# Queries and keys of pairs 2 and 3: one projection and four taps on ScalarE and VectorE instead of four folded weight matrices

## The reference, cut to what matters

```python
def _short_conv(x, w):              # w: 128 channels x 4 taps
    xp = jnp.pad(x, ((0, 0), (3, 0), (0, 0)))
    y = sum((xp[:, t:t + L, :] * w[:, t] for t in range(4)))
    return jax.nn.silu(y)
q = _short_conv(hidden_states @ Wq.T, qconv_w)
k = _short_conv(hidden_states @ Wk.T, kconv_w)
v = _short_conv(hidden_states @ Wv.T, vconv_w)
```

## Time and profile before

| | us |
|---|---|
| three runs: median | 425.53 |
| three runs: lowest, highest | 421.48, 427.27 |
| profiled execution: its own time | 426.13 |
| profiled execution: span, first to last instruction | 424.4 |
| mean granted TensorE clock | 0.918 of full |

### The profile page before, as it was taken

The page is one execution under the profiler, slowest core; times in us unless marked ns, Lnnn a source line. Parts: engine busy times, 40 slices in busy tenths (PEclk is TensorE's granted clock), DMA queues, the critical chain, the costliest instruction groups (busy, mean ns, idle before and its releaser), DMA issues.

```text
span 424.4 us, 14279 instructions
## 1 busy us (share of the span) xinstructions
PE 344.0 (81%) x6364; PEld 253.7 (60%) x6364; DVE 276.2 (65%) x639; ACT 146.2 (34%) x264; POOL 90.2 (21%) x152
## 2 busy tenths in 40 slices
PE   7988977954657796888988869899897987867996
PEld 6344963643324565655776557477675755755885
DVE  3788931268747569767755797498739659667554
ACT  1342613301434351453413413533252353133221
POOL 4862000051622061440200715202000000200000
PEclk9699888968598779999999899899989899899999
DMA  7331350005120001110000011200000000000000
GB/s 255 124 94 29 40 123 19 5 3 129 15 37 4 3 2 28 15 25 14 5 2 2 26 29 15 38 3 3 2 28 4 2 0 0 2 25 2 0 2 25
DMA packets 42652, 12.47 MB, mean 29 GB/s; under 512 B 35424, under 2 KB 41696, under 8 KB 42464
## 3 DMA queue, kind: packets, MB, share of 16 engines
q1 hardware_dynamic: 39440, 9.47, 10.4%
q10 hardware_dynamic: 3152, 2.10, 1.6%
HBM read 8.68 MB, written 2.88 MB: 27 GB/s over the span
## 4 chain that ended last, share of the span: by engine, by line
PE 53%; DVE 24%; issue 8%; DMA 6%; ACT 4%; POOL 4%; SPq 0%; DVEq 0%; ACTq 0%
PE ps L546 17%; PE ps L585 12%; PE ps L441 9%; PE ps L485 7%; PE ps L471 3%; DVE x L1197 2%; DVE v_room L1186 2%; PE ps L614 2%; DMA a_d<-a_hc 2%; DMA t<-t_d 1%; DMA t_d<-t_it 1%; POOL t_it L386 1%; DVE toep_room L1230 1%; PE ps L633 1%; POOL rn L362 1%
## 5 line engine op out<-in xcount | busy, mean ns | idle before, releaser
L1186 DVE TENSOR_TENSOR v_room<-toep_room,ps 128x512 f32<-128x512 f32 x64 | 43.7, 684 | 44.1 <-PE ps L546 20.2
L585 PE MATMUL ps<-w_sb,v_room 128*128 128x128 f32 x512 | 64.9, 281 | 8.9 <-DVE x L1197 4.5
L585 PEld LDWEIGHTS ps<-w_sb,v_room 128*128 128x128 f32 x512 | 62.4, 195 | 14.3 <-issue 8.2
L546 PE MATMUL ps<-x_hi,w_sb 128*128 128x512 f32 x128 | 61.7, 482 | 4.0 <-DVE v_room L1186 2.6
L830 ACT ACTIVATE toep_room<-ps 128x512 f32<-128x512 f32 x64 | 38.1, 597 | 60.1 <-PE ps L546 56.6
L546 PE MATMUL ps<-x_lo,w_sb 128*128 128x512 f32 x128 | 52.4, 409 | 0.0
L546 PE MATMUL ps<-x_hi,w_lo 128*128 128x512 f32 x128 | 52.3, 409 | 0.0
L1197 DVE SCALAR_TENSOR_TENSOR x<-ps,rs,x 128x128 f32<-128x128 f32 x128 | 35.8, 342 | 16.5 <-PE ps L585 16.5
L362 POOL TENSOR_TENSOR rn<-ss,mh 128x16 f32<-128x16 f32 x8 | 23.1, 2901 | 65.1 <-DVE ss L1037 65.1
L396 POOL TENSOR_TENSOR g<-gm,mh 128x16 f32<-128x16 f32 x4 | 11.6, 2909 | 112.2 <-DVE gm L1298 112.2
L546 PEld LDWEIGHTS ps<-x_hi,w_sb 128*128 128x128 f32 x128 | 25.3, 198 | 13.3 <-DVE v_room L1186 3.6
(11 more groups left out here) (199 smaller groups left out, 595.7 us busy)
## 6 DMA issues: line engine op xcount, KB each, us to landing
toep_room<-in_toep SPq DMA_DIRECT2D x1, 1536.0 KB, 12.1
a_d<-a_hc SPq DMA_DIRECT2D x4, 256.0 KB, 3.6
t<-t_d SPq DMA_DIRECT2D x4, 256.0 KB, 3.0
v_room<-in_w SPq DMA_DIRECT2D x1, 1024.0 KB, 6.4
v_room<-in_w ACTq DMA_DIRECT2D x1, 1024.0 KB, 6.6
out_y<-x ACTq DMA_DIRECT2D x4, 256.0 KB, 2.3
taps_room<-in_taps SPq DMA_DIRECT2D x1, 768.0 KB, 5.7
x_sb<-in_x SPq DMA_DIRECT2D x1, 768.0 KB, 8.9
```

The lines of the kernel that those rows point to most:

```text
L546: ins = pe.matmul(bank[:, :], a[cols].bitcast(F32R), c[:, :].bitcast(F32R), start=(k == 0), stop=(k == 2))
L585: ins = pe.matmul(yb[:, P * j:P * j + P], fu[:, e % 2, f, P * j:P * j + P], w2_sb[:, FC * e + f, :], start=(f == 0), stop=(f == FC - 1))
L1186: dve.tensor_tensor(fu[:, e % 2, f, :], sg[:, i % 2, :], ps[VALUE[bank_of(p, i)]][:, :], ALU.mult).then_inc(s["fu_ready"], 1)
```

## The change

For pairs u >= `TAPPED` = 2, so pairs 2 and 3, `conv 0` and `conv 2` multiply x once by the unfolded matrix (`wk_sb`, `wq_sb`), and `conv 1` and `conv 3` do nothing. New steps `k_tap` and `q_tap`: ScalarE copies the PSUM bank into `kf` (`qf`), scaled by the last tap of each channel; VectorE then adds the other three taps, each with one SCALAR_TENSOR_TENSOR that reads the bank shifted by 1, 2 or 3 tokens and updates `kf` in place, with a wait for the one before. Silu then works in place on `kf` (`qf`) and waits for the third of these. The taps come as eight more columns of the `late` load. In `START`, `k_tap` stands behind `conv 1`, ahead of `mix2`, and `k_silu` moves behind `w_out`, for all rounds; `q_tap` stands at the end of the first item of `SCAN`, behind `conv 3`.

```diff
+TAPPED = 2
 START = [("t16t", 0), ("conv", 0), ("mix0", 1), ("t16", 0), ("y_out", 0), *dgv(10), ("mix1", 1), ("dfuse", 10),
-         ("k_silu", 0), ("conv", 1), *dgv(11), ("mix2", 1), ("mix_sq", 1), ("dy", 4), ("dfuse", 11), ("scale0", 1),
+         ("conv", 1), ("k_tap", 0), *dgv(11), ("mix2", 1), ("mix_sq", 1), ("dy", 4), ("dfuse", 11), ("scale0", 1),
          ("t32", 0), ("t32_add", 0), ("vb", 0), ("moved", 0), ("dadd", 4), *dgv(12), ("w", 0), ("w_out", 0),
-         ("k_hc", 0), ("dy", 5), ("dfuse", 12), ("scale1", 1), ("conv", 2), *dgv(13), ("dadd", 5), ("out", 1),
-         ("dfuse", 13)]
-SCAN = [[("ln_cen", 1), ("ln_sq", 1), ("dy", 6), *dgv(14), ("dadd", 6), ("ln_var", 1), ("conv", 3)],
+         ("k_silu", 0), ("k_hc", 0), ("dy", 5), ("dfuse", 12), ("scale1", 1), ("conv", 2), *dgv(13), ("dadd", 5), ("out", 1),
+         ("dfuse", 13)]
+SCAN = [[("ln_cen", 1), ("ln_sq", 1), ("dy", 6), *dgv(14), ("dadd", 6), ("ln_var", 1), ("conv", 3), ("q_tap", 0)],
         [("dfuse", 14), *dgv(15), ("ln_out", 1), ("dfuse", 15)], [("x2t", 1), ("dy", 7), ("dadd", 7)],
...
+                if u >= TAPPED:
+                    if part % 2 == 0:
+                        bank, w, done = ((1, wk_sb, "k_done"), (0, wq_sb, "q_done"))[part // 2]
+                        pe.matmul(ps[bank][:, :], w, xnp[:, bass.ds(u * 2, 2), KS:KS + L],
+                                  start=True, stop=True).then_inc(s[done], 1)
+                    return
...
+            def first_tap(u, bank, done, out, taps):
+                if u >= TAPPED:
+                    act.wait_ge(s[done + "_done"], u + 1)
+                    act.activation(out[:, :, :].rearrange("p m c -> p (m c)"), ps[bank][:, :], ACT.Copy,
+                                   scale=taps[:, 3:4]).then_inc(s[done + "_tap"], 1)
...
             def k_silu(u):
+                if u >= TAPPED:
+                    act.wait_ge(s["k_sum"], (u - TAPPED) * 3 + 3)
+                    act.activation(kf[:, :, :], kf[:, :, :], ACT.Silu).then_inc(s["k_silu"], 1)
+                    return
                 act.wait_ge(s["k_done"], u + 1)
...
+            def other_taps(u, bank, of, out, taps):
+                if u < TAPPED:
+                    return
+                dve.wait_ge(s[of + "_tap"], u - TAPPED + 1)
+                mine = out[:, :, :].rearrange("p (b n) c -> p b (n c)", b=2)
+                have = ps[bank][:, :].rearrange("p (b l) -> p b l", b=2)
+                for back in range(1, 4):
+                    done = (u - TAPPED) * 3 + back
+                    dve.scalar_tensor_tensor(mine[:, :, back:L], have[:, :, 0:L - back], taps[:, 3 - back:4 - back],
+                                             mine[:, :, back:L], ALU.mult, ALU.add).then_inc(s[of + "_sum"], 1)
+                    if back < 3:
+                        dve.wait_ge(s[of + "_sum"], done)
```

More of the change, by code:

```diff
@@ L130, in build @@
         wv_sb, wb_sb, fs_sb = parts(early_sb, D, H, KS)
-        late_sb = sb("late_sb", 3 * D + 2 * HID + 2 + 2 * H * NP + E + 2 * NP + 2)
-        (wq_sb, wk_sb, wo_sb, w1x, w1s, b1_sb, w2r, wg_sb, bias_hc, floor_hc, logt, on_sb) = parts(
-            late_sb, D, D, D, HID, HID, 2, 2 * H * NP, E, NP, NP, 1, 1)
+        late_sb = sb("late_sb", 3 * D + 2 * HID + 2 + 2 * H * NP + E + 2 * NP + 2 + 2 * 4)
+        (wq_sb, wk_sb, wo_sb, w1x, w1s, b1_sb, w2r, wg_sb, bias_hc, floor_hc, logt, on_sb, kw_sb, qw_sb) = parts(
+            late_sb, D, D, D, HID, HID, 2, 2 * H * NP, E, NP, NP, 1, 1, 4, 4)
         taps_room = sb("taps_room", 3 * 4 * D)
@@ L216, in build @@
         fir_done long_ready temp_act temp_vec stats_zero
-        q_done k_done beta_done q_silu k_silu b_tanh bt_ready qk_ready qk_squared ms_ready rn_ready beta_ready kq_ready
+        q_done k_done beta_done k_tap q_tap k_sum q_sum q_silu k_silu b_tanh bt_ready qk_ready qk_squared ms_ready rn_ready beta_ready kq_ready
         kb_ready nbm_ready g_done a_ready attn_ready at_ready aoff_ready a_stored a_items t_items t_stored t16_loaded
@@ L776, in _, with k_tap, q_tap @@
             bank = "p (m t) -> p m t"
+            def first_tap(u, bank, done, out, taps):
[3 more added lines that the diff above has]
+                                   scale=taps[:, 3:4]).then_inc(s[done + "_tap"], 1)
+            def k_tap(u):
+                first_tap(u, 1, "k", kf, kw_sb)
+            def q_tap(u):
+                first_tap(u, 0, "q", qf, qw_sb)
             def k_silu(u):
+                if u >= TAPPED:
+                    act.wait_ge(s["k_sum"], (u - TAPPED) * 3 + 3)
+                    act.activation(kf[:, :, :], kf[:, :, :], ACT.Silu).then_inc(s["k_silu"], 1)
+                    return
                 act.wait_ge(s["k_done"], u + 1)
@@ L783, in q_silu @@
             def q_silu(u):
+                if u >= TAPPED:
+                    act.wait_ge(s["q_sum"], (u - TAPPED) * 3 + 3)
+                    act.activation(qf[:, :, :], qf[:, :, :], ACT.Silu).then_inc(s["q_silu"], 1)
+                    return
                 act.wait_ge(s["q_done"], u + 1)
@@ L919, in body @@
                 steps = {"reload": reload, "sig": gate, "fir": fir, "delta": delta, "square": square, "gelu": hidden, "exp": exp_in, "gelu_set": table(0, ACT.Gelu), "exp_set": table(1, ACT.Exp),
-                         "mix_sq": mix_sq, "moved": moved, "k_silu": beside(k_silu), "q_silu": beside(q_silu),
+                         "mix_sq": mix_sq, "moved": moved, "k_tap": beside(k_tap), "q_tap": beside(q_tap), "k_silu": beside(k_silu), "q_silu": beside(q_silu),
                          "qk_sq": beside(qk_squares), "tanh": tanh, "y_out": y_out, "w_out": w_out, "ln_sq": ln_sq,
@@ L1022, in short_v, with k_tap, q_tap @@
                               f.rearrange("p b l -> p (b l)")).then_inc(s["short_ready"], 1)
+            def other_taps(u, bank, of, out, taps):
+                if u < TAPPED:
+                    return
+                dve.wait_ge(s[of + "_tap"], u - TAPPED + 1)
[7 more added lines that the diff above has]
+                        dve.wait_ge(s[of + "_sum"], done)
+            def k_tap(u):
+                other_taps(u, 1, "k", kf, kw_sb)
+            def q_tap(u):
+                other_taps(u, 0, "q", qf, qw_sb)
             def k_hc(u):
@@ L1396, in body @@
                          "mix1": mix(1), "mix2": mix(2), "scale0": mean_square, "scale1": scale, "out": output,
-                         "t16t": t16t, "vb": v_beta, "t32_add": t32_add, "k_hc": beside(k_hc), "q_hc": beside(q_hc),
+                         "t16t": t16t, "vb": v_beta, "t32_add": t32_add, "k_tap": beside(k_tap), "q_tap": beside(q_tap), "k_hc": beside(k_hc), "q_hc": beside(q_hc),
                          "norms": beside(norms, first if u is not None else None), "beta_hc": beta_hc, "ln_cen": ln_cen,
@@ L1437 @@
                            heads(a["base_bias"]), heads(a["floor_raw"]), heads(a["log_temp"]),
-                           np.tile(a["onorm_w"], H).reshape(P, 1)], axis=1)
+                           np.tile(a["onorm_w"], H).reshape(P, 1), a["kconv_w"].reshape(D, 4), a["qconv_w"].reshape(D, 4)], axis=1)
     taps = np.concatenate([a[n].T.reshape(-1) for n in ("qconv_w", "kconv_w", "vconv_w")])
```

## The result

The changed kernel takes 441.49 us in the median (435.66 to 442.69, 4 runs) against 426.40 before (421.48 to 428.09, 4 runs): a ratio of 1.032, 95% interval 1.017 to 1.047. The forecast was 432.0, 6.5 above the median then known, with a range of 424 to 438. It had the direction right and, for round 0, the place; the measured change, 14 to 15 us, is more than twice as large.

What follows compares the result with a forecast made beforehand. The prediction took VectorE's chain to bound round 0 and TensorE round 1: 426.13 + 6.5 (round 0) + 0.9 (clock) - 0.8 (round 1) = 432.7 us profiled, so 432.0 expected, range 424 to 438.

Steps and rivals of the forecast that it cites:

- What bounds the two places: Round 0 (pair 2): a chain through VectorE; round 1 (pair 3): TensorE nearly full. TensorE relieved of 12.5 us in all.
- Taps 2.34 per tensor: VectorE: three chained SCALAR_TENSOR_TENSORs at 0.78 us each, 2.34 us per tensor.
- k_silu behind w_out: 2.95 of wait, k_hc directly behind silu: Round 0: k_silu queued behind w_out on ScalarE holds k_hc and scale1, 2.95 us beyond the taps' 2.34.
- Table load 1.28 and nothing behind: Round 0, ScalarE: silu's table load starts only after w_out and takes 1.28 us, with no further cost counted.
- rival D: Switching tables costs up to another 1.28 us, delaying silu, k_hc and scale1 of round 0: 433.3 us, chance 0.05.
- w a little longer: Round 0, TensorE: w grows a little at the low clock, within a clock term of +0.9 us.
- the clock +0.9 in all: Round 0: idle TensorE gets the low clock earlier, lengthening w and out: +0.9 us (0 to +3).
- q_tap: 1.2 sticks out: Round 0, VectorE: q_tap's 2.34 us between ln_var and ln_out partly fills a 1.12 us GpSimd wait; 1.2 remains.
- Round 1: -0.8: Round 1 (pair 3): less TensorE work brings x2t earlier, though q_tap delays dfuse 14: -0.8 us.
- Nothing for round 2: Round 2, where nothing is projected: the prediction had no term for it.
- The sum: Whole kernel: 426.13 + 6.5 + 0.9 - 0.8 = 432.7 us for the profiled execution, 432.0 expected.
- C: Rival: taps 1.0 us each, low clock reaching pair 0's first units, round 1 gaining nothing: 437.5 us, chance 0.17.

Runs made afterwards that it cites:

- e7: Changed kernel with a product of all 512 columns, result unused, in place of each removed one: ratio 1.009 to the kernel before.
- e1: Kernel before with only the new order (k_silu behind w_out), all four pairs keeping the folded weights: ratio 0.998 to before.
- e3: Changed kernel with q_tap moved behind ln_out and dfuse 15: ratio 1.024 to the kernel before.
- e8: Changed kernel with k_silu ahead of w_out, q_tap behind ln_out, and an 8-column product for each removed one: ratio 1.005 to before.
- e9: Changed kernel with taps for pair 3 only, its k_silu ahead of w_out, q_tap late, 8-column products for removed ones: 423.70 us, 0.993 to before.
- e6: Changed kernel with a product of 8 columns, result unused, in place of each removed one: ratio 1.018 to the kernel before.
- e10: e9 without its small 8-column products: ratio 1.012 to the kernel before.
- e4: Changed kernel with taps for pair 3 only, in the changed order: ratio 1.020 to the kernel before.
- e12: e4 with small 8-column products in place of the removed ones: round 0 25.6 us, round 2 22.8 us.

## Why the prediction was right or wrong

- *What bounds the two places.* Right for round 0: the chain through VectorE sets the time there. e7 shows it: with TensorE's work given back, 7.6 to 8.3 us of the loss of 8.2 to 9.2 remain, which are the terms below (taps 2.3, k_silu 2.9, q_tap 1.0) and the longer stop in w. That round 1 can pay is argued under *Round 1*.
- *Taps 2.34 per tensor.* Right: 2.31, and mix2 moves by 2.30 against t16t (5.55 from 3.25). That is three of the 0.75 of the earlier trace rows with gaps of 0.03, so reading PSUM at a shift cost nothing more here.
- *k_silu behind w_out: 2.95 of wait, k_hc directly behind silu.* Right in mechanism and price: scale1 moved 7.29 against t16t (17.11 from 9.82), which is 2.3 for the taps, 2.05 for w (next point) and 2.9 for the wait. e1 has the wait alone: scale1 moved by 2.4 with 0.6 of stop less in w, so 3.0. *Table load 1.28 and nothing behind:* right, silu begins 0.01 after the load ends (140.17 against 140.16). That settles rival D for this trace. The drain of about 1380 ns that the Trainium skill's page "ScalarE: Activation LUTs", section "What ACT_TABLE_LOAD costs", adds to the load isn't there, neither in front of the load (w_out ends at 138.87, the load begins at 138.88) nor behind it.
- *"w a little longer"; the clock +0.9 in all.* This is the first step that failed. `out` went from 1.16 to 2.08, the 0.9. But w went from 2.04 to 4.09: 0.8 by the clock, and 1.3 more of standstill at a code border (1.86 against 0.59). The term should have been +3. The range of the term reached that far, for the clock alone; what it had no place for is TensorE standing still for its code.
- *q_tap: 1.2 sticks out.* 1.0 measured (ln_out follows the residual by 5.85 instead of 4.84); moved behind ln_out (e3), it is 4.84 again. Round 0 in all: forecast +7.4, measured +9.2 and, for the second pair of profiles, +8.2.
- *Round 1: -0.8.* Measured 0.0 between the first profiles and +2.5 between the second. Not shown to be wrong, but its spread of 2.6 is larger than the term. In the part that projects, t16t to x_hi, stops at code borders hide it. That part took 30.6 and 29.7 before and 31.0 and 28.7 in the changed kernel; less the stops at its borders (1.1 and 0.5, 2.3 and 0) that is 29.5 and 29.3 against 28.7 and 28.8, so -0.5 to -0.8. By the same count e8 and e9 have 27.8 and 27.7. This is an estimate: it takes each stop to lie on the path.
- *Nothing for round 2.* The second step that failed, by leaving it out: +1.7 and +3.6, from the stop of 2.3 us at the border in w (0.5 and 0 before) and, in the second profile, the lower clock. e6, and e9 against e10, show that the instructions taken out earlier cause the stop; why the clock fell in some of these rounds isn't shown. I had counted removed instructions only as saved time, never as shifted code.
- *The sum.* +9.2 - 0.05 + 1.7 is 10.9, and the spans differ by 9.6: the stretch ahead of round 0 was 1.6 shorter, the one from round 2's x_hi to round 3's 1.3 shorter, and the rest 1.6 longer, with a low clock at 385 to 395 that the profile of before doesn't have there. The change touches none of these three but by the new place of k_silu in round -1. The second profiles give 437.11 against 424.55, +12.6. The medians say +15.1, the ratio's interval 7 to 20; no execution of over 438 us was profiled for this kernel, so the last 1 to 3 us stay open. Of C, whose 437.5 came nearest, the taps at 1.0 us didn't come true. The low level did reach further, to 160 instead of 153.5, but the stretch from round 0's x_hi to round 1's t16t was 51.3 in both kernels. That it came near is luck: the code was not in it.

What stays open: why the code of the border in w of round 0 is asked for late in some programs. In both profiles of before and of e1, and in e9, the packet comes while TensorE waits at the start of w; in e4, e10 and e12, whose programs are the same as e1's or e9's up to there, when w has reached the border or nearly. Also open is what gave e1, and in part e7, the loss of round 0 back.

## What to carry to other kernels

Moving a step one place back in a list that all engines share puts every engine's part of it behind other waits: look, engine by engine, at what now stands ahead of the moved instruction and what is queued behind the one that waits for it. Work taken from the busiest engine is worth something only in the stages where that engine is the late one; here that was at most one of two places, and doing it there alone, with the queue waits repaired and the small products added, is what beat the kernel before, by 0.7%. Where an engine runs streams of hundreds of tiny instructions, its code supply is a resource too: compare the idle times without a releaser at the same instruction number before and after, and try a few small fillers before judging a change that adds or removes instructions. Profile each kernel more than once: the same round of the same kernel changed by up to 2.6 us here from one execution to the next.

## What the runs showed of the hardware that I had not expected

TensorE's code came in packets of 16 KB, and the stops lie at borders 256 instructions of the trace apart. The 128 loads and 128 products of 32x32 of such a step take 1.3 us at the full clock (1.28 for w in e9), and from the packet to the next instruction it took 2.3 us in round 2 of the changed kernel (299.0 to 301.3), and 2.1 to 3.0 at the other stops of all profiles. A piece whose packet comes only at its border costs all of that: in w TensorE stood still for up to 2.8 us while the profile had no releaser to name but "issue". Where the packet had come well before the border there was no stop, as in e9: in the stretch 286 to 288.5 its only packet, for the border after, came at 288.3, and the one for w had come at 284.4 (the window of 283.5 to 286):

```profile
DMA  0000000000000090000000000000000000000000
...
q8 instruction: 1, 0.02, 2.4%
```

A change of 24 instructions in round 1 was worth 2.0 to 3.6 us in round 2, which it didn't touch (e4 against e12; e10 against e9, with the clock of the round at 0.94 in e10).
